# Feed-forward of a spline network: gate and up contracted over 128 moments of the tokens, the attention mask written into PSUM by ScalarE

## What is computed

```python
# attention
q, k, v = x @ wq.T, x @ wk.T, x @ wv.T            # 16 heads of 16
scores = einsum('bihd,bjhd->bhij', q, k) * scale
mask = idx[None, :] - idx[:, None] > WINDOW // 2   # key over 16 ahead of the query
attn = softmax(where(mask, -inf, scores))
out = einsum('bhij,bjhd->bihd', attn, v) @ wo.T
# feed-forward
w = 0.5 * (2.0*p1 + (p2-p0)*f + (2.0*p0-5.0*p1+4.0*p2-p3)*f2 + (3.0*p1-p0-3.0*p2+p3)*f3)
gate = einsum('bsh,ih->bsi', hidden, gate_w)       # 256 -> 1024
up = einsum('bsh,ih->bsi', hidden, up_w)
out = einsum('bsi,hi->bsh', silu(gate) * up, down_w)
```

## Time and profile before

| | |
|---|---|
| median of three runs | 590.39 us |
| lowest, highest | 589.18, 593.07 us |
| profiled execution, span | 587.0 us |
| PE, PE weight loads | 573.4 us (98%), 501.5 us (85%) |
| DVE | 505.7 us (86%) |
| ACT, POOL | 243.3 us (41%), 207.6 us (35%) |
| chain that ended last | PE 88%, DVE 9% |
| costliest PE groups | `ga` and `up`, 1536 matmuls |
| mean granted PE clock | 0.991 |

### The profile page before, as it was taken

The page is one execution under the profiler, slowest core; times in us unless marked ns, Lnnn a source line. Parts: engine busy times, 40 slices in busy tenths (PEclk is TensorE's granted clock), DMA queues, the critical chain, the costliest instruction groups (busy, mean ns, idle before and its releaser), DMA issues.

```text
span 587.0 us, 13711 instructions
## 1 busy us (share of the span) xinstructions
PE 573.4 (98%) x5402; PEld 501.5 (85%) x5402; DVE 505.7 (86%) x1029; ACT 243.3 (41%) x369; POOL 207.6 (35%) x249
## 2 busy tenths in 40 slices
PE   7899999999999999999999999999999999999997
PEld 6466689898998988889898888989888888988997
DVE  4998999989799898999989899899998998886642
ACT  2324634443343434444434434344443444443422
POOL 4742623333241423342242324323232324333332
PEclk9789999999999999999999999999999999999999
DMA  8451421213023131111313121222212202101000
GB/s 255 123 178 52 134 74 58 90 56 110 11 72 101 56 108 49 62 57 55 108 57 109 57 75 42 67 91 74 92 56 68 69 29 74 55 21 38 1 19 20
DMA packets 44415, 42.87 MB, mean 73 GB/s; under 512 B 4544, under 2 KB 43072, under 8 KB 44352
## 3 DMA queue, kind: packets, MB, share of 16 engines
q1 hardware_dynamic: 44352, 41.99, 22.4%
HBM read 12.35 MB, written 4.19 MB: 28 GB/s over the span
## 4 chain that ended last, share of the span: by engine, by line
PE 88%; DVE 9%; issue 2%; POOL 1%; ACT 0%; DVEq 0%; POOLq 0%
PE ring L720 15%; PE ring L721 13%; PE ring L722 13%; PE ring L802 8%; PE ring L727 8%; PE ring L729 7%; PE ring L728 7%; PE pair L770 7%; PE pair L794 5%; DVE M L655 2%; PE ring L711 2%; DVE W L611 1%; PE ring L742 1%; PE ring L748 1%; DVE Z L634 1%
## 5 line engine op out<-in xcount | busy, mean ns | idle before, releaser
L559 ACT ACTIVATE P<-pair 128x800 f32<-128x800 f32 x128 | 106.2, 836 | 131.1 <-PE pair L794 130.6
L720 PE MATMUL ring<-YT,WGUh 128*128 128x256 f32 x512 | 151.7, 296 | 0.0
L722 PE MATMUL ring<-YT,WGUl 128*128 128x256 f32 x512 | 144.5, 282 | 0.0
L721 PE MATMUL ring<-YT,WGUh 128*128 128x256 f32 x512 | 144.3, 282 | 0.0
L655 DVE TENSOR_REDUCE M<-pair 128x2 f32<-128x288 f32 (+1 forms) x256 | 134.3, 569 | 4.2 <-PE pair L779 0.6
L515 POOL TENSOR_TENSOR IN<-GU,IN 128x512 fp32r<-128x512 f32 x64 | 82.4, 1287 | 133.0 <-ACT IN L520 132.8
L720 PEld LDWEIGHTS ring<-YT,WGUh 128*128 128x128 f32 x512 | 96.5, 188 | 6.7 <-issue 2.2
L721 PEld LDWEIGHTS ring<-YT,WGUh 128*128 128x128 f32 x512 | 96.6, 189 | 0.0
L507 POOL TENSOR_SCALAR_AFFINE_SELECT P<-P 128x448 f32<-128x448 f32 x64 | 37.9, 592 | 165.5 <-ACT P L559 165.5
L722 PEld LDWEIGHTS ring<-YT,WGUl 128*128 128x128 f32 x512 | 96.3, 188 | 0.0
L649 DVE TENSOR_TENSOR pair<-pair,UP 128x512 f32<-128x512 f32 x104 | 71.4, 686 | 7.8 <-PE pair L770 7.6
(11 more groups left out here) (80 smaller groups left out, 1071.0 us busy)
## 6 DMA issues: line engine op xcount, KB each, us to landing
QM<-QK SPq DMA_DIRECT2D x96, 128.0 KB, 2.1
KS<-QK SPq DMA_DIRECT2D x96, 128.0 KB, 2.1
X<-x SPq DMA_DIRECT2D x32, 256.0 KB, 3.0
out<-X SPq DMA_DIRECT2D x16, 256.0 KB, 2.3
OVER<-over SPq DMA_DIRECT2D x4, 256.0 KB, 6.7
P<-wqk SPq DMA_DIRECT2D x2, 256.0 KB, 4.8
TAP<-points SPq DMA_DIRECT2D x2, 256.0 KB, 4.7
POWER<-powers SPq DMA_DIRECT2D x2, 256.0 KB, 5.7
```

What stands on the lines that cost most here:

```text
L559: nc.scalar.activation(P[:, g % 2, 2 * (n % 2):2 * (n % 2) + 2, :], pair(what, t, n)[:, :, 0:SW], ACT.Exp, scale=SCALE).then_inc(exp_done, 1)
L720: mm(o, wh[:, kb, c], act[:, 0, kb, :], start=j == 0 and kb == 0, stop=False, skip_group_check=True)
L721: mm(o, wh[:, kb, c], act[:, 1, kb, :], start=False, stop=False, skip_group_check=True)
L722: i = mm(o, wl[:, kb, c], act[:, 0, kb, :], start=False, stop=False, skip_group_check=True)
```

## The change

**Gate and up.** Hidden units are put in a new order (`tile_rows`) in eight tiles of 128, and the tiles in three groups (OF_TILE: 3, 3 and 2 tiles), so that within a group all rows of a matrix cross from one cubic to the next inside the same two short stretches of features (`segments`). Over such a stretch a feature is kept as it is, by a unit vector; over the long stretches between, each row of the matrix is one cubic of the feature's index, and the features are first contracted with four constant cubics (`whole_cubics`, `moment_tables`). This gives at most 128 numbers a token, the moments, in place of 256 features. The constant table TM (256 x 3 x 128) comes from DRAM. A new step `mo` forms the moments of a turn from YT: `mo` 0 those of groups 0 and 1 (8 matmuls), `mo` 1 those of group 2 (4). TM needs no low part, so two matmuls a block. ACT copies the moments to a high part, DVE subtracts for the low part, into Y (double). `ga` and `up` then take one block of 128 in place of two: 6 matmuls a step in place of 12. YT is single now.

```diff
+        for lo, hi, v, direct in segments(g):
+            p = np.arange(lo, hi)
+            if direct:
+                turned[p, g, m + p - lo] = 1.0
...
+                m += hi - lo
+            elif hi > lo:
+                cubics = whole_cubics(hi - lo)
+                turned[lo:hi, g, m:m + 4] = cubics.T
+                rows[:, g, 1, m:m + 4] = (np.linalg.pinv(cubics.T) @ piece(p, v)).T
+                m += 4
```

```diff
-                elif what in ("ga", "up"):
-                    pe.wait_ge(ws_low, 4 if n < 2 else 8)
-                    pe.wait_ge(z2_low, nth("z2", t, 0))
-                    m = ("ga", "up").index(what)
-                    columns(bk, (2 * n * 128, 2 * n * 128 + 128), WGUh[:, m], WGUl[:, m], YT[t % 2],
-                            (ga_made, up_made)[m])
+                elif what == "mo":
+                    pe.wait_ge(tm_done, 1)
+                    pe.wait_ge(z2_low, nth("z2", t, 0))
+                    for g in (2,) if n else (0, 1):
+                        o = bk[:, (0 if n else g) * S:(0 if n else g) * S + S]
+                        for kb in range(KB):
+                            mm(o, TM[:, kb, g, :], YT[:, 0, kb, :], start=kb == 0 and g != 1, stop=False, skip_group_check=True)
+                            i = mm(o, TM[:, kb, g, :], YT[:, 1, kb, :], start=False, stop=False, skip_group_check=True)
+                    i.then_inc(mo_made, 1)
+                elif what in ("ga", "up"):
+                    pe.wait_ge(ws_low, 2 if n < 2 else 4)
+                    pe.wait_ge(mo_low, nth("mo", t, 0 if n < 3 else 1))
+                    m = ("ga", "up").index(what)
+                    y = Y[t % 2]
+                    for j in range(2):
+                        o, g = bk[:, j * S:(j + 1) * S], OF_TILE[2 * n + j]
+                        wh, wl = (w[:, m, (2 * n + j) * 128:(2 * n + j + 1) * 128] for w in (WGUh, WGUl))
+                        mm(o, wh, y[:, 0, g, :], start=j == 0, stop=False, skip_group_check=True)
+                        mm(o, wh, y[:, 1, g, :], start=False, stop=False, skip_group_check=True)
+                        i = mm(o, wl, y[:, 0, g, :], start=False, stop=False, skip_group_check=True)
+                    i.then_inc((ga_made, up_made)[m], 1)
```

ACT's and DVE's parts of `mo`, and ACT's copy in `z2`, which now waits for the `mo` of the turn before:

```diff
+                elif what == "mo":
+                    act.wait_ge(mo_made, nth("mo", t, n))
+                    if t == 0 and n == 0:
+                        act.wait_ge(permuted, 24 * DMA)
+                        act.wait_ge(ws_low, 4)
+                    if t >= 2 and n == 0:
+                        act.wait_ge(up_made, nth("up", t - 2, 3))
+                    g = slice(2, 3) if n else slice(0, 2)
+                    copy(Y[t % 2][:, 0, g, :], moments(bank(what, t, n), n)).then_inc(mo_high, 1)
...
+                elif what == "mo":
+                    dve.wait_ge(mo_high, nth("mo", t, n))
+                    low(Y[t % 2][:, 1, g, :], moments(bank(what, t, n), n), Y[t % 2][:, 0, g, :]).then_inc(mo_low, 1)
```

```diff
+                elif what == "pm":
+                    sp.wait_ge(ws_sum, n + 5)
+                    if n == 0:
+                        sp.wait_ge(ws_over, 4)
+                        sp.wait_ge(tapped, 2)
+                    m, c = chunk(n + 4)
+                    for half in range(2):
+                        a = 8 * (m - 2) + 4 * c + 2 * half
+                        for g in range(3):
+                            nt, j0 = TILES[g], OF_TILE.index(g)
+                            sp.dma_start(WP[8 * a:8 * a + 16, j0:j0 + nt, :],
+                                         W[2 * BEGIN[g]:2 * BEGIN[g] + 16 * nt, n, half * D:(half + 1) * D]).then_inc(permuted, DMA)
...
+                elif what == "wd":
+                    act.wait_ge(permuted, 24 * DMA)
+                    copy(WD[:, 2 * n:2 * n + 2, 0:D], WP[:, 2 * n:2 * n + 2, :]).then_inc(wd_high, 1)
```

```diff
+                elif what == "sd":
+                    if t == 0 and n == 0:
+                        act.wait_ge(seed_loaded, DMA)
+                        act.wait_ge(heated, 1)
+                    if BEFORE["s1", t, n]:
+                        act.wait_ge(*emptied(BEFORE["s1", t, n]))
+                    copy(pair("s1", t, n)[:, :, 0:SW], SEED[:].unsqueeze(1).broadcast_to([128, 2, SW])).then_inc(seeded, 1)
-                if BEFORE.get((what, t, n)):
+                if what == "s1":
+                    pe.wait_ge(seeded, nth("sd", t, n))
+                elif BEFORE.get((what, t, n)):
                     pe.wait_ge(*emptied(BEFORE[what, t, n]))
-                                   start=it == 1, stop=it == 0 and t >= EARLY, skip_group_check=True)
+                                   start=False, stop=it == 0, skip_group_check=True)
-                    if t >= EARLY:
-                        edge = pr[:, :, AHEAD:AHEAD + 384].rearrange("p a (i j) -> p a i j", j=128)[:, :, 0:3:2, :]
-                        tt(edge, edge, UP[:].rearrange("p (i j) -> p i j", i=2).unsqueeze(1).broadcast_to([128, 2, 2, 128]),
-                           ALU.add).then_inc(masked, 1)
-                        dve.wait_ge(masked, nth("s1", t, n) - EARLY * NP)
```

350 lines of the change are left out of this document (214 added, 136 removed), and 248 rows, old and new, of tables (OWN, START, TURN).

## The result

| | before | after |
|---|---|---|
| median of four runs | 589.78 us | 546.09 us |
| lowest, highest | 587.80, 593.07 | 541.96, 547.26 |
| profiled execution, span | 587.0 | 545.4 |
| PE busy | 573.4 (98%) | 516.1 (95%) |
| DVE, ACT busy | 505.7, 243.3 | 440.6, 362.1 |

The ratio is 0.9244, 95% interval 0.9191 to 0.9297: the kernel is 44 us faster. The forecast was 520 us, 26 us too low, and the range (507 to 542) did not hold the result. One execution in all that follows was a slow one, over 1.5% above the fastest of its kernel (`w1_fill_waits`, 549.48 us); it is in that kernel's median and not in its ratio.

What follows compares the result with a forecast made beforehand. TensorE was taken to bound the kernel, at 0.120 us a matmul. From 587.0: -92.2 +23.0 (gate and up, `mo`) -7.7 -5.3 (mask, spline) +5 +7 +3 (seeds, head, tail) -3.2 (`av`) gives 516.6, +3.4 gives 520 us; range 507 to 542.

Steps and rivals of the forecast that it cites:

- The seed: ACT writes the mask, 128x800, into two PSUM banks before the score matmuls add to them: 0.84 us each, 128 times.
- The 0.2 us a turn for `av`: `av` groups standing two and two save two changes of tiling a turn, 0.1 us each: 3.2 us in 16 turns.
- Seeds late in the turns: In steady turns, two places where PE waits for ACT's mask write, late together by 0.15 us: +5 us in 16 turns.
- Tail: Last turn, a chain: `mo` adds a link on PE, ACT and DVE: +3 us, bounds 0 and 8.
- Median over span: Median of the runs lies 3.4 us above the profiled span, as before the change: 516.6 becomes 520 us.
- I take a third, +7: Head: late mask writes and SP's transfers against a saving of 13 us; bounds 0 to 21 worse (nothing gained, 8 lost).
- the 7.7 and 5.3 us saved: PE work leaving the head: 7.7 us of mask writing in turns 0 to 2, 5.3 us of spline-chunk matmuls.
- Turn 0's `mo` waits for all 24: Head: `mo` of turn 0 waits for SP's 24 permuting transfers, 15.4 us of its queue, hidden by turn 0's attention.
- rival 3: Late seeds make gaps in every turn, PE's clock falls to half and the kernel gets slower, 675 us: chance 0.04.
- The spline chunks: Head: four of twelve chunks go, with 8 matmuls at 0.66 us each: 5.3 us less of PE.
- the head grows: Late seeds and SP's 24 transfers take the 14 us left of the head's bounds: 534 us, chance 0.10.
- The first (a turn of 31 us): ACT and DVE set the steady turn together, 31.0 us in place of 29.6: 542 us, chance 0.18.

Runs made afterwards that it cites:

- w1_fill_waits: Changed kernel plus 72 matmuls that do nothing, put into three places where PE waited in the head: 541.51 us, ratio 0.9171 to the kernel before.
- h1_head_order: Changed kernel with seven due times of the head moved back toward the old order and the first two seeds issued later: 546.79 us, ratio 0.9281.
- y3_permute_later: Changed kernel with the third group of six permuting transfers behind turn 2's first `ld`, and the first two down-weight splits later: 539.65 us, ratio 0.9192.
- x3_pe_mask_1: Changed kernel, but PE writes the mask in turn 0 and ACT's seeds begin after it: 541.50 us, ratio 0.9207 to the kernel before.
- m1: Changed kernel with the old mask: PE writes it in turns 0 to 2, DVE adds it after, no seeds: 581.96 us, ratio 0.9864.
- all repairs: Changed kernel with PE's mask in turn 0, later permuting transfers, GpSimd's memsets held for turn 1's layernorm, and 54 idle matmuls: 533.35 us, ratio 0.9059.
- z1: Kernel before, with 6 matmuls without a use at the start in place of 26: 592.10 us against 589.08, ratio 1.0067.
- the parts: New gate and up with the old mask on the changed kernel, 581.96 us; ACT's seeds alone on the kernel before, 627.36 us.
- p1_memset_waits: Changed kernel with GpSimd's memsets of the second slots waiting for DVE's layernorm scaling of turn 1: 543.08 us, ratio 0.9181.

## Why the prediction was wrong

**What held.** A `ga` matmul costs 0.120 us, and `ga` and `up` have half as many. The steady turn: 29.46 us forecast, 29.47 measured, 298 instructions, PE without idle time. DVE: 26.7 forecast, 26.01 measured; ACT: 22.3 forecast, 22.13 measured. The seed: 0.84 us taken from the exponential's row, 0.842 measured. All of this had been worked out from rows of other instructions on the same engine. The 0.2 us a turn for `av` don't show: 33.78 - 29.47 is the 4.31 of gate and up alone.

**Seeds late in the turns** (+5): the steady turn shows no idle time of PE, so this term is close to nothing. PE's reaction in it, 0.2 us, had no row; after, a seed ends at 77.29 and its scores start at 77.34.

**Tail** (+3): from the last wo to the last sum 24.6 us (517.45 to 542.07) in place of 26.3, 1.7 less where the sum took 4.3 off for that turn's gate and up; behind that wo PE is idle 6.5 us in place of 3.4. So the term was about right.

**What else lies behind turn 4.** This part is 2.6 us longer than forecast, though its share of the seeds (3.8) was not used. The turns 5 to 12 gave what they should (234.9 us in place of 269.5, 4.33 a turn). The three behind them gave 8.6 (wo of turn 12 to wo of turn 15: 75.97 us in place of 84.56) in place of 13, with PE idle 2.5 us in place of 0.5: where the turns run out, the sum had no term.

**Median over span** (+3.4): here it is 0.7, as the profiled execution was the slowest of four. That leaves 28.8 us missed in the span as 26.1 in the median.

**What failed is the head**: "I take a third, +7", with bounds of 0 and 21. The two rows for it measure 28.8 us, past the upper bound. And of the 13 us saved, from which it was counted, 5.3 were not there. The bound was a sum of three things that I saw (8 us of late issues and the 7.7 and 5.3 us saved) and it left out these:

1. *The wait costed at nothing.* "Turn 0's `mo` waits for all 24, hidden by the attention of turn 0." `mo` did not pay; what stands behind those 24 on SP did: the `ld` of turns 1 and 2, behind them ACT's copies into the tile that they read, behind these the seeds, behind these PE's scores. I followed the first six of the 24 (to the second `ld` of turn 0) and stopped there. In `h1_head_order` that `ld` goes 7 us earlier, in an edit of seven due times, and nothing is gained; in `y3_permute_later` the third group and the splits behind the 24 go later, and 3 to 6 us are.
2. *The clock in the head.* I had it as rival 3, for the turns, and put the low clock "in the head alone", as if it were free there. It costs 12 to 19 us of the 28.8. I held against the turns only and not against the new head; the head after has 48 and 60 matmuls in its first two stretches where that of before has 62 and 103. The sign that I had named for a wrong forecast, a clock of 0.5 past the head, has its trace in the stretch from 80 to 100 us (0.70, mean of 20 us).
3. *VectorE behind GpSimd.* The scaling of turn 1's layernorm was held some 4.5 us behind GpSimd's row of operations. No row of before shows this at its full size; there the same two instructions took 2.35 us at 22.86, beside GpSimd's operations, against 0.41 each later (mean of 12 between 200 and 400 us), and that was to be seen.
4. *The seeds of turn 0*, of score steps that follow one another: 2 to 5 us by `x3_pe_mask_1`. I had worked the places of the seeds out for the steady turn alone.
5. *The spline chunks, sized wrongly.* "Three of these are six PE rows of together 1.98, 0.66 each: 5.3 us of PE": the price was read from one place, and I took it that the chunks that stay keep it. Before, two matmuls ran side by side where their steps met; after, most of the last ones stand alone. 48 rows at 0.31 us before and after: the term is about nothing.

**Rivals.** The second, "the head grows", named the right place; its sign to look for was "the first steady turn hardly earlier than before", and the sum of turn 4 comes at 206.5 against 203.3. At 534 us and 0.10 it was too small and too unlikely: it filled the gap to my bound and had no mechanism for the clock. The first (a turn of 31 us) did not come; the kernel with DVE's mask kept (`m1`) shows what it would have looked like: DVE 30.75 of 32.53 us. The third has its mechanism shown and its place wrong.

**What stays open.** With all repairs the first sum of turn 4 comes at 191.8 us. By the terms of the forecast without its 7 us for the head it would come at 173.4; the added matmuls (9.1), 3.2 us more of idle time than before (12.7 against 9.5) and 1.5 less through the clock make 184.2, and with the 5.3 us of the chunks 189.5. Of the 2.3 us that remain the 12 matmuls of `dn` are 1.4; in the kernel after the same count is 1.9 us too high, so it is good to some 2 us. It is not settled how far the clock and the waits can be told apart: most edits that took a wait away raised the clock with it, and only `z1` moved one alone. So the 28.8 us of the head are shown as idle time and low clock, but how they divide among the causes above is shown only roughly: the sizes of the single edits are as large as their uncertainty.

## What to carry to other kernels

Cost the head of a pipelined kernel by its own list of waits, not as a fraction of a bound: for each transfer that is added to an in-order queue, follow what stands behind it through every engine until TensorE, and see in which stretches TensorE then does less than it did where its clock was low. When one edit frees an engine and another uses it, measure them together, since here the parts gave -7 and +38 us apart and -44 together. Take a matmul's price from the place where it will stand: a matmul of 32 rows beside a neighbour cost half of what it cost alone here. Once the steady turn is right, look at the first turns: four small edits there (order of transfers, one wait, 54 idle matmuls, the mask of one turn) gave a further 13 us.

## What the hardware showed that I had not expected

- A VectorE instruction of 0.58 us lasted until GpSimd paused: two took 5.72 us (one of them 4.95) beside four operations of GpSimd without a gap, and 2.23 us when the third of these waited. An addition of VectorE that read PSUM took its 0.69 us beside the same work (at 27.93 us; at 26.58 in `p1_memset_waits`). The Trainium skill (SBUF — State Buffer, "Who interferes with whom") has one pair of ports that both engines use, locked for a whole instruction, and lists `tensor_scalar` among those that can take it, when their operands meet the conditions. The trace agrees on who is held; it was held past the end of several instructions of GpSimd, not one.
- ScalarE wrote 128x800 to PSUM in 842 ns (128 times) and read as much from there in 837. The Trainium skill (ScalarE: Activation LUTs, "Step-by-step: what each stage is for") has a write to PSUM as the faster one; these rows show no such gain, though they are not a clean pair, as the one reads bf16 from SBUF and the other fp32 from PSUM.
- The low clock cost 0.27 us for each us (between executions of one kernel, and about as much in `z1_before_less_hot`), not 0.5, and the record of it can fail: 1.00 in `z1_before_less_hot`, where the matmuls stand 0.21 us apart. The distance between matmuls is the safer reading.
- Two fp32 matmuls from different 32-row slices ran side by side when their steps met: 1.06 us for both, where one alone takes 1.05.
